# Order of the tree levels and of their weight loads in a fused GNN, attention and tree-FFN kernel

## What is computed

```python
for i in range(DEPTH + 1):              # levels 0..7
    nodes_i = all_nodes[i]
    t_i = jnp.einsum('td,tdo->to', flat_x, w2s[nodes_i]) + b2s[nodes_i]
    out = out + t_i * path_weights[:, i][:, None]
...
x = x + _L0_ffn_ref(_layernorm(x, axis=-1)[None], L0_ffn_w1s, L0_ffn_b1s, L0_ffn_w2s, L0_ffn_b2s)[0]
```

## The kernel before, in words

| level | pairs | units | units with a fixed node |
|---|---|---|---|
| 1 | 1 | 9 | 2 |
| 2 | 2 | 9 | 4 |
| 3 | 4 | 9 | 8 |
| 4 | 8 | 13 | 12 |
| 5 | 16 | 21 | 20 |
| 6 | 32 | 37 | 36 |
| 7 | 64 | 69 | 68 |
| sum | 127 | 167 | 150 |

## Time and profile before

### The profile page before, as it was taken

The page is one execution under the profiler, slowest core; times in us unless marked ns, Lnnn a source line. Parts: engine busy times, 40 slices in busy tenths (PEclk is TensorE's granted clock), DMA queues, the critical chain, the costliest instruction groups (busy, mean ns, idle before and its releaser), DMA issues.

```text
span 423.3 us, 9132 instructions
## 1 busy us (share of the span) xinstructions
PE 363.4 (86%) x2530; PEld 260.8 (62%) x2533; DVE 258.0 (61%) x697; ACT 142.8 (34%) x451; POOL 109.8 (26%) x226
## 2 busy tenths in 40 slices
PE   0699899998699999929694999999999997777877
PEld 0466668996588888818562556666666563333555
DVE  2646769951916060574897568787878674445531
ACT  1345463100103223023610025555555553333410
POOL 6200005000000000344103024554455554333420
PEclk9999976555699999977898899999999999999989
DMA  7921138302999000000072024799999999999101
GB/s 214 251 63 39 36 81 229 98 4 70 375 386 386 25 0 2 1 0 1 2 247 100 2 64 173 280 339 379 387 386 386 384 385 386 386 387 379 39 2 61
DMA packets 51783, 78.45 MB, mean 185 GB/s; under 512 B 3260, under 2 KB 19223, under 8 KB 51736
## 3 DMA queue, kind: packets, MB, share of 16 engines
q1 hardware_dynamic: 50506, 76.81, 52.5%
q10 hardware_dynamic: 1230, 1.05, 0.9%
HBM read 77.21 MB, written 0.64 MB: 184 GB/s over the span
## 4 chain that ended last, share of the span: by engine, by line
PE 70%; DVE 11%; SPq 6%; DMA 6%; issue 3%; ACT 3%; DVEq 1%; POOLq 0%; POOL 0%; ACTq 0%
PE ps L1204 67%; SPq L392 5%; DMA reg<-in_L_ffn_w2s_dram 3%; DMA reg<-in_L_gnn_Wc_dram 2%; PE ps L1207 2%; DVE reg L937 1%; DVE reg L811 1%; DVE reg L931 1%; DVE reg L1147 1%; DVE reg L971 1%; DVE stats L982 1%; DVE reg L1198 0%; ACT reg L685 0%; DVE acc L979 0%; SPq L368 0%
## 5 line engine op out<-in xcount | busy, mean ns | idle before, releaser
L1204 PE MATMUL ps<-reg 128*64 128x256 f32 (+5 forms) x1447 | 260.5, 333 | 6.5 <-DVE reg L1193 2.5
L1204 PEld LDWEIGHTS ps<-reg 128*64 128x64 f32 (+5 forms) x1449 | 176.6, 166 | 22.3 <-issue 4.9
L1204 PE MATMUL ps<-reg,reg_w 128*64 (+1 forms) x688 | 162.7, 388 | 16.6 <-issue 8.1
L1204 PEld LDWEIGHTS ps<-reg,reg_w 128*64 128x64 f32 (+1 forms) x688 | 91.8, 139 | 78.0 <-issue 35.9
L533 POOL TENSOR_TENSOR reg_w<-reg_w 128x128 f32 x150 | 75.8, 505 | 99.6 <-ACT reg_w L712 78.6
L1147 DVE SCALAR_TENSOR_TENSOR reg_w<-reg_w,nid,reg 128x128 f32 x167 | 63.6, 385 | 47.2 <-PE ps L1204 43.3
L711 ACT COPY reg_w<-ps 64x128 f32<-64x128 f32 x150 | 39.4, 263 | 97.0 <-PE ps L1204 84.1
L1147 DVE SCALAR_TENSOR_TENSOR reg<-reg_w,reg 128x128 f32 x150 | 50.6, 338 | 0.4 <-issue 0.2
L712 ACT COPY reg_w<-ps 64x128 f32<-64x128 f32 x150 | 39.2, 261 | 3.6
L811 DVE TENSOR_TENSOR reg<-iota,idxH 125x660 bf16<-125x660 f16 (+5 forms) x42 | 38.7, 988 | 0.0
L1207 PE MATMUL ps<-ident,reg 128*128 128x128 f32 (+4 forms) x78 | 15.1, 319 | 21.8 <-DMA reg<-in_L_gnn_We_dram 12.5
(11 more groups left out here) (241 smaller groups left out, 263.4 us busy)
## 6 DMA issues: line engine op xcount, KB each, us to landing
reg<-in_L_ffn_w2s_dram SPq DMA_DIRECT2D x127, 512.0 KB, 11.4
reg<-in_edge_attr_dram SPq DMA_DIRECT2D x13, 336.0 KB
reg<-in_L_gnn_Wc_dram SPq DMA_DIRECT2D x3, 512.0 KB, 9.5
reg<-in_L_gnn_Wn_dram SPq DMA_DIRECT2D x3, 256.0 KB, 5.8
xin<-in_x_dram ACTq DMA_DIRECT2D x1, 512.0 KB
out_dram<-reg SPq DMA_DIRECT2D x4, 128.0 KB
reg<-in_edge_attr_dram SPq DMA_DIRECT2D x13, 39.0 KB
reg<-in_L_mix_w_qkv_dram ACTq DMA_DIRECT2D x1, 384.0 KB, 7.4
```

The costliest lines, as they stand in the source:

```text
L1204: return e.matmul(to, lhsT, rhs, start=start, stop=stop, skip_group_check=True)
```

## The change

The levels are run in the order 7, 3, 2, 6, 5, 1, 4 by every engine, and the pairs are loaded in that order too (`ORDER`, `PLACE`, `PAIR0`). Offsets that were lists over the levels are now sums over the levels that come earlier in `ORDER`. Where the parity or the number of a level chose a buffer or a semaphore's count, its place t in the order now does. The ranks are spread during level 6 (`RR`) instead of level 7, to a place of their own (`vec_b`, which holds four bias and gain vectors that are used up by then). The five operations on `PmT` stand in level 5 behind its units 8, 11, 14, 17 and 20, where they stood in level 7 behind 48, 52, 56, 60 and 64. The number of loads, units, matmuls, masks, copies and additions is the same.

```diff
+ORDER = (7, 3, 2, 6, 5, 1, 4)
+PLACE = {l: t for t, l in enumerate(ORDER)}
...
+BASE = {l: sum(UNITS[m] for m in ORDER[:PLACE[l]]) for l in SORTED}
+BASE2 = {l: sum(len(FIXED[m]) for m in ORDER[:PLACE[l]]) for l in SORTED}
+PAIR0 = {l: sum(2 ** (m - 1) for m in ORDER[:PLACE[l]]) for l in SORTED}
...
+RR = 6
+PMT_AT = ((5, 8), (5, 11), (5, 14), (5, 17), (5, 20))
...
-        gamma_b = sb("gamma_b", [128, D])
-        beta_b = sb("beta_b", [128, D])
-        gout_b = sb("gout_b", [128, D])
-        bout_b = sb("bout_b", [128, D])
+        vec_b = sb("vec_b", [128, 4 * D])
+        gamma_b, beta_b, bout_b, gout_b = (vec_b[:, v * D:(v + 1) * D] for v in range(4))
...
-        rank_row = part(reg_m, 0, 128, R)
+        rank_row = vec_b[:, 0:R]
...
         def last_step(p):
 
-            l = (p + 1).bit_length()
+            l = level_of(p)
             if MOVED[l] == 0:
-                return BASE[l + 1]
-            return BASE[l] + max(p + 1 - 2 ** (l - 1) + 6, HEAD + 1)
+                return BASE[l] + UNITS[l]
+            return BASE[l] + max(p - PAIR0[l] + 6, HEAD + 1)
...
             def pair(p):
-
+                l = level_of(p)
+                n0 = 2 ** l - 1 + 2 * (p - PAIR0[l])
                 e.dma_start(ring[:, p % PAIRS, :].rearrange("p (n c) -> p n c", n=2),
-                            w2s[1 + 2 * p:3 + 2 * p].rearrange("n (p k) d -> p n (k d)", p=128)
+                            w2s[n0:n0 + 2].rearrange("n (p k) d -> p n (k d)", p=128)
...
-                if b == BASE2[LEVELS - 1] + 6:
+                if b == BASE2[RR] + 12:
                     e.wait_ge(p_rr, 1)
                     e.copy(rank_row[:, 0:4 * TP], ps[:, 7, :]).then_inc(s_rr, 1)
-                if b == BASE2[LEVELS - 1] + 12:
+                if b == BASE2[RR] + 17:
                     e.wait_ge(p_rr, 2)
...
-                    if k == 3 and l == LEVELS - 1:
+                    if k == 8 and l == RR:
                         e.tensor_tensor(rdiag, ident[:, :].unsqueeze(1).broadcast_to([128, NT, TP]),
...
-                    if l == LEVELS - 1 and k in range(48, 48 + 4 * NT, 4):
-                        w = (k - 48) // 4
+                    if (l, k) in PMT_AT:
+                        w = PMT_AT.index((l, k))
                         e.wait_ge(s_rr, 2)
                         e.wait_ge(made, MADE["rowid"])
                         e.wait_ge(used, last_step(PAIRS * 3 + 3))
...
+                    if k == 1 and t == PLACE[RR] + 1:
+                        e.wait_ge(s_rr, 2)
...
-                        e.wait_ge(*loads_of(2 ** (l - 1) - 1 + p))
+                        e.wait_ge(*loads_of(PAIR0[l] + p))
...
-                    if l == LEVELS - 1 and k in (4, 9):
-                        n = (4, 9).index(k)
+                    if l == RR and k in (9, 14):
+                        n = (9, 14).index(k)
```

More of the change, by code:

```diff
@@ L54 @@
 SORTED = range(1, LEVELS)
[L55 to L61, removed]
+ORDER = (7, 3, 2, 6, 5, 1, 4)
+PLACE = {l: t for t, l in enumerate(ORDER)}
+FIXED = {l: [n for n in range(2 ** l) if n < HEAD or n % 2] for l in SORTED}
+MOVED = {l: 2 ** l - len(FIXED[l]) for l in SORTED}
+UNITS = {l: MOVED[l] + NW - 1 for l in SORTED}
+BASE = {l: sum(UNITS[m] for m in ORDER[:PLACE[l]]) for l in SORTED}
+BASE2 = {l: sum(len(FIXED[m]) for m in ORDER[:PLACE[l]]) for l in SORTED}
+PAIR0 = {l: sum(2 ** (m - 1) for m in ORDER[:PLACE[l]]) for l in SORTED}
+U = sum(UNITS.values())
+U2 = sum(len(f) for f in FIXED.values())
+COLS = {l: slice(BASE[l], BASE[l] + UNITS[l]) for l in SORTED}
+RR = 6
+PMT_AT = ((5, 8), (5, 11), (5, 14), (5, 17), (5, 20))
 HALF = ((0, 512), (512, R))
@@ L488, in _ @@
             for l in SORTED:
-                ins = e.memset(first[:, COLS[l]], float(2 ** l - 2))
+                ins = e.memset(first[:, COLS[l]], float(2 * PAIR0[l]))
                 if l < LEVELS - 1:
@@ L522, in _ @@
             c.wait()
-            for l in SORTED:
+            for l in ORDER:
                 n = len(FIXED[l])
@@ L705, in _ @@
             sorted_tokens(3)
-            for b in range(BASE2[-1]):
+            for b in range(U2):
                 e.wait_ge(used2, b + 1)
@@ L1161, in _ @@
                         e.wait_ge(used, u - NLHS + 1)
-                    masked(lhs[:, u % NLHS, :, :], l, within(offs[u % RU] & 1023, (NW - 1) * WIN), nid[:, u:u + 1]).then_inc(lhs_full, 1)
+                    masked(lhs[:, u % NLHS, :, :], t, within(offs[u % RU] & 1023, (NW - 1) * WIN), nid[:, u:u + 1]
+                           ).then_inc(lhs_full, 1)
                     if k < len(FIXED[l]):
@@ L1166, in _ @@
                             e.wait_ge(used2, b - NLHS + 1)
[L1167 to L1172, removed]
-                    if k == 3 and l == LEVELS - 1:
+                        masked(lhs2[:, b % NLHS, :, :], t, within(offs[u % RU] >> 10, (NW - 1) * WIN), float(FIXED[l][k])
+                               ).then_inc(lhs2_full, 1)
+                    if k == 3 and t < len(ORDER) - 1:
+                        level_rows(t + 1, 0)
+                    if k == 6 and t < len(ORDER) - 1:
+                        level_rows(t + 1, 1)
+                    if k == 8 and l == RR:
                         e.tensor_tensor(rdiag, ident[:, :].unsqueeze(1).broadcast_to([128, NT, TP]),
@@ L1494, in _, with spread @@
                ).then_inc(p_pre, 1)
[L1496 removed]
+            def spread(t, n):
                 c0, c1 = HALF[n]
[L1499 to L1502 removed]
+                if t > 0:
+                    e.wait_ge(spread_read, 2 * t + n + 2)
+                mm(ps[:, (5 if t == 0 else 3) + n if t < 1 else 7, 0:c1 - c0], sel[:, ORDER[t] if t >= 0 else 0, :],
+                   leaf_rows[:, c0:c1], True, True).then_inc(p_spread, 1)
             e.wait_ge(s_rows, 1)
@@ L1505, in _ @@
             e.wait_ge(tabs_u, TABS["nodes"])
-            for l in range(2):
+            for t in (-1, 0):
                 for n in range(2):
-                    spread(l, n)
+                    spread(t, n)
             e.wait_ge(s_sort, 4)
@@ L1517, in _ @@
             e.wait_ge(tabs_u, TABS["addresses"])
-            for l in SORTED:
+            for t, l in enumerate(ORDER):
                 for k in range(UNITS[l]):
@@ L1522, in _ @@
                         at = registers(tab_pe[0:1, u:min(u + RU, U)], mybir.EngineType.PE, TOP_PE)
-                    if k == 1 and l < LEVELS - 1:
-                        spread(l + 1, 0)
-                    if k == 4 and l < LEVELS - 1:
-                        spread(l + 1, 1)
+                    if k == 1 and t == PLACE[RR] + 1:
+                        e.wait_ge(s_rr, 2)
+                    if k == 1 and t < len(ORDER) - 1:
+                        spread(t + 1, 0)
+                    if k == 4 and t < len(ORDER) - 1:
+                        spread(t + 1, 1)
                     second = k < len(FIXED[l])
```

45 lines of the change are left out of this document (21 added, 24 removed).

## The result

| | before | after |
|---|---|---|
| median, us | 426.51 (4 runs, same chip) | 415.41 (4 runs) |
| lowest, highest, us | 425.64, 427.36 | 414.60, 416.52 |
| profiled execution, us | 425.05 | 415.6 |
| its span, us | 423.3 | 413.9 |

The ratio is 0.9741, with a 95% interval from 0.9711 to 0.9772. The forecast was 416 us.

The account below looks back on a forecast made before the run. The weight stream was taken as the bound late in the tree, with about 21 us of waiting in level 7. Gains of 10.0 (order) and 0.6 (POOL) gave execution 414.5, plus 1.7 for a median: 416, range 411 to 421.

Parts of the forecast that it names:

- The stream: Weight loads from pair 32 on: unbroken from 243.4 us instead of 281.05, at 1.355 us a pair.
- Rival D: Loads: the unbroken stream doesn't start at 243 us, tree end stays within 2 us of 405, time 425; 6%.
- The landing constant: Loads: 6.4 us added to stream start plus 1.355 us a pair; at the least half, 3.2 us less.
- No wait in level 7: Level 7: PE fully busy from about 243 to 295 us; a wait there would count against the forecast.
- 8.9 us of slack: Level 6, unit 27: PE could reach it at 336.1 us but is held for pair 101 until 345.0.
- The levels without waits: Behind level 5's unit 11: 8.63 us of level 5, 8.54 of level 1, 11.2 of level 4, none held up.
- the lag of 7.5 us: Level 7: POOL's additions, 0.98 us each, end 7.5 us behind PE's unit 67; covered by buffers, costed at nothing.
- The tail: End of the tree: POOL's last addition follows the last copy by 0.76 us instead of 1.34, gain 0.6.
- A: Levels 5, 1 and 4: late DVE hand-overs eat half the gain, tree ends at 399 to 400, time 420 to 421; 15%.
- C: Whole tree: POOL becomes the bound, slower than before above 1.14 us an addition; 448 us if DVE and POOL exclude each other; 5%.
- Rival B: Whole tree: PE is the only bound, tree ends at 384 to 390, time 405 to 411; 5%.
- The sum: Whole kernel: 10.0 us from the tree plus 0.6 from POOL's end, 10.6 less, execution from 425.05 to 414.5.

Follow-up runs that it names:

- falling: Changed kernel with levels in the order 7, 6, 5, 4, 3, 2, 1 and the PmT operations in levels 5 and 4: 423.32 us, ratio 0.9927.
- one_first: Changed kernel with level 1 moved to the front (1, 7, 3, 2, 6, 5, 4): 416.83 us, ratio 0.9794.
- one_early: Changed kernel with level 1 moved before level 6 (7, 3, 2, 1, 6, 5, 4): 413.39 us, ratio 0.9708.
- ranks_only: Changed kernel with the old level order 1 to 7 and the PmT operations back in level 7: 425.6 us, ratio 0.999.
- pmt_twice: Changed kernel with each of the five PmT operations done twice, with a wait between: 415.62 us, ratio 0.9767.
- half_after: Changed kernel with each load from pair 32 on bringing only the first matrix of its pair (incomplete result): 404.89 us, ratio 0.9521.
- pool_odd: Changed kernel with POOL's address reads in level 7 moved to units 0, 9, 21, 33, 45 and 57: 414.21 us, ratio 0.9749.
- half_before: Kernel before with each load from pair 32 on bringing only the first matrix of its pair (incomplete result): 412.8 us, ratio 0.9701.
- one_early_even: Changed kernel in the order 7, 3, 2, 1, 6, 5, 4, with POOL's address reads cut to start on multiples of 4: 410.82 us, ratio 0.965.

## Why the prediction held, and where it didn't

**The stream.** Shown. Pair 32 goes out at 243.49 us, the rate is unbroken to 372 us, and 512 KB at that rate are 1.36 us a pair. `falling`, `one_first` and `one_early` moved the start and the units behind the last wait separately, and the time followed both. `ranks_only` showed that the spread of the ranks and its new place add nothing measurable, and `pmt_twice` that the operations on `PmT` are covered in their new place. Rival D is out.

**The landing constant: the step that was off.** "Landing = start + 6.4 + 1.355 x number of pairs" was sized from the old stream and used for one that is longer. Unit 11 of level 5 started at 368.19, not 366.6: with 0.3 for the hand-over and 86 x 1.355 from 243.4 the constant is 7.9 to 8.0. It isn't constant. By the same working pair 61 (289.56) gives 5.2, pairs 100 and 101 (344.22, 345.54) give 7.0, pairs 110, 116 and 117 (358.68, 366.80, 368.19) 7.9. The old stream had done the same, from the landings in its trace: 2.4 at pair 47, 4.6 at the pairs 79 to 92, 5.5 from pair 93 and 6.4 from pair 113 on. Landings come 1.35 us apart except at single pairs (61, 79, 95 and 109 here), where they come 0.8 to 1.0 us later; in the mean that is 0.05 us a pair. The end of the stream suggests why: with all loads issued by 368.42 us, the share of the 16 DMA engines and the rate fall off step by step (windows as above), and the last pair lands only at 380.75.

```profile
375.00:376.00 1.00, 1.00 (x12) 0.66 (x9) 1.00 (x5) 0.59 (x3) 0.52 (x1) 1.00 0.60 217
...
377.00:378.00 1.00, 1.00 (x9) 0.43 (x6) 0.18 (x1) 0.02 (x1) 0.48 (x1) 1.00 0.11 37
```

So some of the engines were about 5 us behind the others, and if a pair has landed only when the last of them has brought its part, landings fall behind the mean rate; that was not tried. The cost was 1.5 us, which is 396.55 against 395.0. My bound for this term went the wrong way only: I asked whether 6.4 was too much, never whether it grows with the length of the stream.

**No wait in level 7: wrong.** I named a wait there as a sign against the forecast, and it came. I checked the landing times for levels 6 and 5 alone. Pair 53 by my own form lands at 243.4 + 6.4 + 22 x 1.355 = 279.6, while PE reaches its unit 49 at 243.1 + 40 x 0.863 = 277.6; pair 63 lands at 293.2, for unit 59 at 286.3. So the term for level 7, 60 x 0.863 us after 243.1, left out a wait of 7 us by my own form. The window from 277 to 294 us lacks 3.9 us of PE. ACT's copies in it show the stream's pace, with idle times before them that level 7 didn't have earlier:

```profile
279.12 0.26 ACT L720 COPY reg_w<-ps 64x128 f32<-64x128 f32 x1 [0.55 <-PE ps L1215]
...
292.07 0.26 ACT L720 COPY reg_w<-ps 64x128 f32<-64x128 f32 x1 [0.81 <-PE ps L1215]
293.42 0.26 ACT L720 COPY reg_w<-ps 64x128 f32<-64x128 f32 x1 [0.79 <-PE ps L1215]
```

The first copy of level 3 comes at 302.68, and at 296.07 in `half_after`, which never waits: the wait in level 7 takes 6.6 us. It cost nothing in the sum, since PE was held again later, in level 6, and had 8.9 us of slack up to there; only about 2 were left. The wait at unit 27 of level 6 ends at 345.54 where I had 345.0. Of the 11.15 us by which the last copy comes later than in `half_after` (396.01 against 384.86), 6.6 arise in level 7, 1.1 in level 6 and 3.5 in level 5. In `one_early` the 5.2 us of level 7 are all that the stream still costs.

**The levels without waits.** Levels 3, 2 and 1 took 8.54, 8.54 and 8.53 us, as worked out. From 368.19 to the end were 28.4 us, for which I had 8.63 + 8.54 + 11.2 = 28.4. Two matmuls for the ranks, at units 9 and 14 of level 6, were missing from my sum. `half_after`, where nothing hides them, needs 34.5 us for level 6 instead of 33.16, so about 1.3 us, which lie under the wait in the changed kernel.

**POOL.** The 0.98 us an addition in level 7 did not come: POOL kept PE's pace with a lag of 0.76 us behind the copies, at most 1.14, because all reads of that level begin at multiples of 4 here. So the lag of 7.5 us that I costed at nothing wasn't there to be covered. That such a lag is covered, up to the 6.8 us behind PE that it reached there, is shown by `pool_odd`, at 0.2 us of PE. The tail was right: 0.57 us for 0.6.

**Rivals A and C.** A (late hand-overs in short levels) is refuted by the last window, in which PE is busy for all of its 27.6 us, and by `pmt_twice`. C needed 1.14 us an addition. In the densest stretch, level 7 of `half_after` from 245.03 to 295.11 us, POOL did 58 additions at one every 0.863 us, beside two masks of DVE per unit. The lock between DVE and GpSimd that the Trainium skill states ("SBUF: two separate sides" in SBUF — State Buffer) would have made that 1.10 by the rows of before; no run here shows the two excluding each other to that extent. In the first window of the changed kernel DVE is busy for 26.23 and POOL for 19.35 of 34.00 us, so for at least 11.6 us both are. POOL can be the bound of this tree, as `half_before` indicates, but by costly reads of addresses.

**Rival B.** PE alone as the bound is what `half_after` shows, whose tree ends at 385.4, and `one_early` from 292 us on. In the change itself the stream is a bound too.

**The sum.** Forecast: 10.0 for the tree and 0.6 for POOL, 10.6. Measured: 8.45 and 0.57, and 0.4 behind them that I hadn't counted (the clock in the permutation), 9.4 in the profiles. For the profiled execution I forecast 414.5 and 415.6 was measured, 1.1 us more. To get a median I then added 1.7 us, by which the median of before lay above its profiled execution; in the changed kernel it lies 0.2 below. The two errors have opposite signs, so that 416 met the median of 415.41 within 0.6 us is partly luck.

## What to carry to other kernels

When a ring of buffers feeds an engine, the time is the start of the unbroken stream, plus its length, plus the work behind the last transfer that is waited for: put first the part that gives buffers back one by one, and last what needs little work, and place compute without loads where it is held up anyway. Check every stage against the landing times, not only the last ones, and take the lag of a long stream from its end. A cost that seems to belong to an operation, such as reading addresses, may belong to where its data begins; look at two places at which it differs.

## What the runs showed that was unexpected

- POOL's read of 12 addresses from a table in SBUF takes a step of 1.07 to 1.09 us between additions where it begins at a multiple of 16 bytes from the table's start and POOL isn't held by something else, and 2.97 to 3.02 where it doesn't. The additions themselves take 0.46 us in the median in either case.
- A stream at a steady 386 GB/s doesn't deliver each pair at that pace: the landings fall behind in jumps of 0.8 to 1.0 us, from 5.2 us at pair 61 to 7.9 at pair 117. The cause was not tried.
- PE's granted clock in the permutation is 1.00 in the changed kernel, 0.86 in the one before, and 0.84 over the 11 us in both kernels with level 1 before level 6. PE's idle time ahead of it doesn't sort these cases: it was 1.91 us in the changed kernel and 2.48 in `one_first`, both at 1.00, and 1.91 in `one_early_even` and 2.54 in `one_early`, both at 0.84. In `one_early` the lower clock costs 0.6 us of what the earlier end of the tree brings: 12.4 us from DVE's first addition to PE's end (391.94 to 404.32) instead of 11.8 (397.33 to 409.09). What decides it stays open.
